# The inverse y step with its four quarters in another order: a Fourier tower on one Trainium2 core

## What is computed

```
for i in range(nl):
    h_ft = jnp.fft.rfft2(h)
    w_c = spec_wr[i] + 1j * spec_wi[i]
    out_modes = jnp.einsum('bixy,ioxy->boxy', h_ft[:, :, :mx, :my], w_c)
    spec = jnp.fft.irfft2(out_modes, s=(H, W))
    conv = lax.conv_general_dilated(h, conv_w[i], (1, 1), 'SAME', dimension_numbers=dn)
    conv = conv + conv_b[i][None, :, None, None]
    h = leaky(spec + conv)
```

## Time and profile before

| what | value |
|---|---|
| median of 3 runs | 1127.58 us (1126.82 to 1130.13) |
| span of the profiled execution | 1127.1 us |
| PE busy | 1056.2 us, 94% |
| DVE, ACT, POOL busy | 604.8, 464.6, 152.8 us |
| PE's share of the chain that ended last | 85% |

### The profile page before, as it was taken

The page is one execution under the profiler, slowest core; times in us unless marked ns, Lnnn a source line. Parts: engine busy times, 40 slices in busy tenths (PEclk is TensorE's granted clock), DMA queues, the critical chain, the costliest instruction groups (busy, mean ns, idle before and its releaser), DMA issues.

```text
span 1127.1 us, 48730 instructions
## 1 busy us (share of the span) xinstructions
PE 1056.2 (94%) x22512; PEld 562.8 (50%) x22512; DVE 604.8 (54%) x560; ACT 464.6 (41%) x895; POOL 152.8 (14%) x299
## 2 busy tenths in 40 slices
PE   5899899899999999899999998999999999899985
PEld 2655554555455544645555555434444443366743
DVE  5687788645556656555556665201233213377844
ACT  3355555223333333133334342233453434566424
POOL 2021211011111111011111110102102021210000
PEclk9999999999999999999999999999999999999998
DMA  9287668478988888488899887578667363000001
GB/s 319 67 213 213 191 173 243 130 215 254 258 241 250 251 215 248 133 244 256 252 261 265 240 232 192 141 164 196 167 146 167 93 148 83 5 6 1 1 1 19
DMA packets 66714, 194.27 MB, mean 172 GB/s; under 512 B 22256, under 2 KB 24816, under 8 KB 59248
## 3 DMA queue, kind: packets, MB, share of 16 engines
q1 hardware_dynamic: 54224, 138.19, 45.4%
q0 software_dynamic: 12288, 52.97, 16.8%
HBM read 138.13 MB, written 52.95 MB: 170 GB/s over the span
## 4 chain that ended last, share of the span: by engine, by line
PE 85%; DVE 6%; issue 5%; ACT 4%; DMA 0%; DVEq 0%; ACTq 0%
PE psum L662 16%; PE psum L648 14%; PE psum L694 11%; PE psum L676 7%; PE psum L620 6%; PE psum L633 5%; PE psum L566 4%; PE psum L553 4%; PE psum L712 3%; PE psum L605 2%; PE psum L903 2%; PE psum L720 1%; DVE xt L1283 1%; DVE ft L1289 1%; DVE spec L1401 1%
## 5 line engine op out<-in xcount | busy, mean ns | idle before, releaser
L1092 ACT ACTIVATE x_now<-psum,conv_bias 128x512 f32<-128x512 f32 x256 | 155.4, 692 | 323.5 <-PE psum L676 249.9
L1312 DVE STREAM_TRANSPOSE vt<-psum 128x1024 f32<-128x1024 f32 x64 | 126.5, 1977 | 205.2 <-PE psum L620 205.2
L1283 DVE STREAM_TRANSPOSE xt<-x_now 128x1024 f32<-128x1024 f32 x100 | 199.5, 2034 | 14.9 <-ACT x_now L1092 8.7
L1289 DVE STREAM_TRANSPOSE ft<-psum 128x1024 f32<-128x1024 f32 x50 | 100.3, 2007 | 190.3 <-PE psum L553 190.3
L662 PE MATMUL psum<-halo,conv 64*32 64x512 f32 x3072 | 190.3, 593 | 5.6 <-issue 5.4
L346 ACT ACTIVATE spec<-psum 32x128 f32<-32x128 f32 x372 | 143.9, 387 | 95.1 <-PE psum L566 91.2
L648 PE MATMUL psum<-halo,conv 128*128 128x512 f32 x384 | 178.0, 605 | 0.7 <-ACT x_now L1092 0.7
L497 POOL DMA_DIRECT2D activations<-x_now x192 | 94.4, 492 | 605.4 <-PE psum L662 411.9
L694 PEld LDWEIGHTS psum<-dft,vt 64*64 64x64 f32 x8192 | 126.5, 135 | 49.9 <-issue 49.9
L694 PE MATMUL psum<-dft,vt 64*64 64x64 f32 x8192 | 136.1, 220 | 2.0 <-issue 1.9
L648 PEld LDWEIGHTS psum<-halo,conv 128*128 128x128 f32 x384 | 68.5, 188 | 84.1 <-issue 75.2
(11 more groups left out here) (158 smaller groups left out, 796.1 us busy)
## 6 DMA issues: line engine op xcount, KB each, us to landing
halo<-activations SPq DMA_DIRECT2D x768, 132.0 KB, 3.5
activations<-x_now POOLq DMA_DIRECT2D x192, 264.0 KB, 4.3
wspec<-in_spec SPq DMA_DIRECT2D x64, 256.0 KB, 5.7
xcol<-in_xcol SPq DMA_DIRECT2D x16, 384.0 KB, 5.2
x_now<-in_ser SPq DMA_DIRECT2D x2, 1024.0 KB, 6.6
spec<-in_onehot SPq DMA_DIRECT2D x8, 256.0 KB, 5.7
wspec<-in_causal SPq DMA_DIRECT2D x8, 256.0 KB, 6.3
consts<-in_tail SPq DMA_DIRECT2D x6, 185.0 KB, 5.7
```

The source lines that it names most:

```text
L1092: copy(x_now[:, k, 16 * u:16 * u + 16, 0:G], acc[u].rearrange("p (i j) -> p i j", j=G), ACT.Prelu, bias=conv_bias[:, l:l + 1], alpha=SLOPE ...
L1283: vec.transpose(xt[:, 32 * m:32 * m + 32, :], src).then_inc(s_xt, 1)
L1289: vec.transpose(ft[:].rearrange("p k c -> p c k"), rowed.rearrange("p a b -> p (a b)").rearrange("p (i c) -> p c i", c=C)).then_inc(s_ft, 1)
L1312: vec.transpose(vt[:, k].rearrange("p h r o -> p (h r) o").rearrange("p y o -> p o y"), backed.rearrange("p a b -> p (a b)").rearrange("p ...
```

## The change

In `columns_back` the four quarters are issued in the order 0, 2, 1, 3 in place of 0, 1, 2, 3. The products, their operands and the signal on the last of them are the same.

```
                 pe.wait_ge(s_zt, 4 * l + 4)
                 reached(pe, s_vt, T)
-                for m in range(4):
+                for m in (0, 2, 1, 3):
                     il, ri = m // 2, m % 2
                     for h in range(2):
                         for cg in range(2):
```

## The result

The changed kernel takes 1121.14 us, the median of 20 runs (1110.23 to 1127.2), beside 1128.99 us of the kernel before in 20 runs. The ratio is 0.9914 with the 95% interval 0.9896 to 0.9933: 9.7 us faster, 7.6 to 11.7. (The ratio and its interval come from the fast runs, which leave out the one at 1127.2; they are not the quotient of the two medians, which is 0.9930.) Applied to the 1127.58 us shown before the forecast, the ratio gives 1117.9 us; the forecast was 1117.2, a ratio of 0.9908.

What follows compares the result with a forecast made beforehand. PE, the matmul engine, busy 94% of the span, was the bound. Savings of 5.3 + 2.8 + 1.1 + 0.6 + 0.6 = 10.4 us took 1127.1 to 1116.7; adding 0.5 gave 1117.2 us, 80% range 1113.5 to 1122.5.

Steps and rivals of the forecast that it cites:

- The price of a block: Inner L620 block, start to next step: 0.70 us plus 0.31, so 1.01 us instead of 1.24, saving 0.23.
- L676's stagger: L676's eight tiles start within about 0.05 us of each other; the same was taken for L620's first turn.
- The upper bound: L620 block time of 1.06 us, from the block at 225.44 after a wait; total forecast then 1119.3 us.
- The sum by layer: L620 savings: layers 1 and 2 5.3 us, layer 3 2.8, layer 0 without gaps 1.1.
- The blocks whose tiles come late: Layers 1 and 2: two with half their tiles late still save 0.23 us; five others, as at 371.85, save nothing.
- The block with a pause: Layer 0 at 168.66: 13 records left after a pause spread over eight tiles instead of four, saving 0.4 us.
- The layer boundaries: Three blocks, as at 222.00: L620 ends 0.2 us sooner, so VectorE and the waiting block follow; 0.6 us together.
- What is late next: Waits behind L620: L566's ft transpose keeps 0.38 us of margin, none closes, so no gain is counted as lost.
- Sixteen records stand ahead: L620 block start: sixteen records for the first four tiles precede the other four's first; those idle about one turn.
- Rival 1: L620 records start strictly in program order, so the swap brings nothing: 1127.6 us, chance 0.10.
- The rule of the Trainium skill: Matmuls on PE start and end strictly in program order; by it the forecast would be no change.
- The rival of pauses: PE pauses with no releaser, as on L662, take back the gain: 1124 to 1128 us, chance 0.05.

Runs made afterwards that it cites:

- e8: Kernel before, old quarter order; in inner pairs of layers 1 and 2 the block stands behind L566 instead of ahead; 1143.01 us, ratio 1.012.
- e6: Changed kernel reordered so five products on the first four tiles stand ahead of the first for the other four; 1119.6 us, ratio 0.9900.
- e4: Changed kernel reordered so six products on the first four tiles stand ahead of the first for the other four; 1129.4 us, ratio 0.9994.
- e5: Changed kernel reordered by strip and row half, quarters 0, 2, 1, 3 within each, eight records in a row on two tiles; 1130.55 us, ratio 1.0012.
- e7: Changed kernel reordered so seven products on the first four tiles stand ahead of the first for the other four; 1132.47 us, single run.

## Why the prediction was right

The forecast was 1117.2 us in a range of 1113.5 to 1122.5; the ratio gives 1117.9 for the same runs of before, and the median as measured is 1121.14. The steps, by their own numbers:

- The price of a block. Forecast 1.01 us from start to the next step for 1.24, by L676's stagger. Measured 1.01, in both profiles, and 0.70 from first to last start in the trace's records, where the kernel before has 0.94. The upper bound came from the block at 225.44 with 1.06 us; the one that answers to it takes 1.03 in the new order (227.78 to 228.81), so the blocks after a wait save 0.03 where nothing was forecast.
- The sum by layer. Forecast 5.3 us for layers 1 and 2, measured 2.8 + 2.6 = 5.4 in busy time; layer 3 2.8 against 2.9; layer 0 1.1 against 1.2.
- The blocks whose tiles come late. At 313.64, the block that answers to the earlier trace rows, L566 starts 1.54 us after the first record where it was 1.78 (from 314.13), so it saves 0.24; at 370.10 it starts 1.56 us after it, as from 371.68 to the 373.24 of the earlier trace rows: nothing saved. Timeline of the changed kernel:

```profile
313.64 0.41 PE L620 MATMUL psum<-zt,dft 64*32 64x256 f32 x4
...
315.18 0.54 PE L566 MATMUL psum<-dft,ft 128*32 128x64 f32 x24
```

```profile
370.10 0.42 PE L620 MATMUL psum<-zt,dft 64*32 64x256 f32 x6
...
371.66 0.54 PE L566 MATMUL psum<-dft,ft 128*32 128x64 f32 x24
```

- The block with a pause. 19 records, then 13, as in the earlier trace rows, but the 13 now take 0.66 us in place of 1.06: 0.4 us, as forecast. Timeline:

```profile
166.47 1.02 PE L620 MATMUL psum<-zt,dft 64*32 64x256 f32 x19
168.01 0.66 PE L620 MATMUL psum<-zt,dft 64*32 64x256 f32 x13 [0.52 <-issue]
```

- The layer boundaries. Here a term was too large: forecast 0.2 us each, measured 0.12. From the start of the first block to that of the second are 3.32 us, and they were 3.44:

```profile
224.46 1.07 PE L620 MATMUL psum<-zt,dft 64*32 64x256 f32 x32
...
227.78 1.10 PE L620 MATMUL psum<-zt,dft 64*32 64x256 f32 x32 [0.53 <-DVE vt L1312]
```

 The block's last record ends 0.20 us sooner after the block's start, but VectorE takes the result up 1.18 us after it (224.46 to 225.64) where it was 1.31 (222.00 to 223.31), only 0.13 sooner: its transpose follows the recorded end by 0.11 us in place of 0.04, at all three boundaries and in both profiles of the changed kernel. Why it does stays open; it is 0.25 us in all.
- What is late next. No wait came in place of the gain: L566's waits for ft are 4.5 us in 7 cases in both profiles of the changed kernel, and 4.5 us in 7 cases before.

Two things in the prediction's reasons were vague and held by luck of the margin. "Sixteen records stand ahead" was taken for the cause without a measure of how far PE sees; the runs give it, 33 to 36 instructions behind L676, so five products ahead would have done, and six would not. And it was read as a matter of what the block itself holds; e8 shows that the step ahead decides too.

Rival 1 (records start strictly in the order of the program) is refuted by the result as by the earlier trace rows: the order changed the time, and records overtake one another. The rule of the Trainium skill, "TensorE: Matmul & The Clock Gate", section on packing small matmuls, which the prediction named beside it, would have left the time as it was; the traces disagree with it.

The rival of pauses is not borne out as a cost of the change. The single runs of the changed kernel spread over 17 us, more than the change is worth, and the longer ones tend to have the lower mean granted clock (1127.2 us at 0.984, 1110.23 at 0.994). That fits pauses of varying length with the half clock behind a long one, but only one of these 20 executions has a trace, so it is not shown. A single pair of profiles would have given 6.6 us, or with the second 12.4.

## What to carry to other kernels

When products stand on small tiles of the array, what counts is how many different tiles the stretch of program reaches that PE has in sight: here 33 to 36 instructions behind a step of 512-column records, and at least 45 where nothing older was left. That is in line with 64 places less those that the step ahead still holds. A product of this type takes four. Put the products of a step so that each tile appears once before any tile appears twice, at the least at the start of the step. One tile out of sight cost a whole turn here, nearly as much as three, so a partial reordering can bring nothing (six products ahead) or everything (five).

## What the runs showed of the hardware

- The stretch of the program that PE works on out of order ends sharply: the tile whose first load is number 33 started in the first turn (e6, e4, e5), the one with number 37 didn't (e4, e7, e5), behind a step of 512-column records. That agrees with 64 places, of which 29 were still held by L676, a count that was worked out and not measured by itself. In e8, where nothing older was left, all eight tiles started, the last with load number 45.
- Places come free late. In e4 the eighth tile's first matmul starts some 0.2 us after the others, though the tile was idle. That fits places that are given back only when an older record is complete, and a record is shown for 0.16 us longer (0.376 us) than its turn of 0.215. This reading was argued, not tested by itself.
- PE paused with no releaser at the same record of its program in every trace (0.69 to 3.35 us at the last record of one block of layer 0).
- After PE had stood still for 3.35 us, the granted clock was 0.50 in a stretch of 6.6 us, and four records of L633 took 3.78 us in place of 1.98.
